# One transpose instead of two for the score maxima of a batch, and two VectorE additions in place of one

## The reference, cut to what matters

```python
v = (ctx @ Wv + bv); k = (ctx @ Wk + bk); q = (layernorm(x) @ Wq + bq)   # each cut into 16 heads of 16
energy = einsum('nqhd,nkhd->nhqk', q, k)
energy = where(mask == 0, neg, energy)
attn = softmax(energy / sqrt(16), axis=-1)
out = einsum('nhqk,nkhd->nqhd', attn, v).reshape(N, 128, 256) @ Wo + bo
x = x + tanh(g_xattn) * out
x = x + tanh(g_ffn) * tanh(layernorm(x) @ weight @ aux1 @ aux2 + bias)
```

## Time and profile before

| | |
|---|---|
| time, median of 3 runs | 1120.8 us (1119.55 to 1123.22) |
| span of the profiled execution, first to last instruction | 1118.3 us |
| TensorE busy | 1073.6 us, 96% of the span, 18979 products and transposes |
| VectorE busy | 966.1 us, 86% |
| ScalarE busy | 826.3 us, 74% |
| GpSimd busy | 774.2 us, 69% |
| granted TensorE clock, mean over the span | 0.988 of full speed |

### The profile page before, as it was taken

How to read it: one execution, slowest core, us unless ns; L and a number is a source line. 1 busy time by engine, 2 the same in 40 slices (tenths; PEclk the granted TensorE clock), 3 DMA queues, 4 the chain that set the end, 5 groups by cost and what they waited for, 6 DMA issues and landing times.

```text
span 1118.3 us, 45477 instructions
## 1 busy us (share of the span) xinstructions
PE 1073.6 (96%) x18979; PEld 941.8 (84%) x18979; DVE 966.1 (86%) x1272; ACT 826.3 (74%) x1275; POOL 774.2 (69%) x1185
## 2 busy tenths in 40 slices
PE   5989999999999999999999999999999999999975
PEld 4777888888888888888888888888888888888865
DVE  4788888988988988898888898898889889889876
ACT  4465877877887787787777787778778778777842
POOL 5245677777777776776777777777777777777653
PEclk9899999999999999999999999999999999999997
DMA  6134344334434433433433443443443344343232
GB/s 167 30 89 117 77 120 136 102 106 134 110 114 119 128 107 107 135 108 98 136 103 104 136 108 112 123 124 106 112 135 106 102 135 108 113 121 108 71 116 77
DMA packets 160189, 124.78 MB, mean 112 GB/s; under 512 B 91889, under 2 KB 126962, under 8 KB 159986
## 3 DMA queue, kind: packets, MB, share of 16 engines
q1 hardware_dynamic: 159842, 121.61, 38.8%
q10 hardware_dynamic: 144, 0.26, 0.1%
HBM read 69.41 MB, written 51.38 MB: 108 GB/s over the span
## 4 chain that ended last, share of the span: by engine, by line
PE 89%; DVE 5%; issue 2%; SPq 2%; DMA 1%; ACT 0%; DVEq 0%
PE ps_m L455 17%; PE ps_m L448 16%; PE ps_s L573 13%; PE ps_s L546 12%; PE ps_x L585 11%; PE ps_m L510 8%; PE ps_m L442 5%; PE ps_s L552 4%; PE ps_x L563 2%; DVE neg_max L938 2%; DVE probs L949 2%; DMA a_rows<-scratch_a 0%; DMA den<-a_den 0%; SPq L200 0%; PE ps_m L598 0%
## 5 line engine op out<-in xcount | busy, mean ns | idle before, releaser
L949 DVE TENSOR_TENSOR probs<-ps_s,far_T 128x2048 f32<-128x2048 f32 x128 | 293.3, 2292 | 36.8 <-PE ps_s L573 36.6
L938 DVE TENSOR_REDUCE neg_max<-ps_s 128x16 f32<-128x2048 f32 x128 | 291.3, 2276 | 6.4 <-PE ps_s L552 6.3
L748 ACT ACTIVATE probs<-probs 128x2048 f32<-128x2048 f32 x128 | 244.5, 1910 | 7.9 <-DVE probs L949 7.7
L723 ACT ACTIVATE q_aug<-ps_m,q_bias,q_scale 128x256 f32<-128x256 f32 x256 | 123.7, 564 | 161.9 <-PE ps_m L448 152.4
L573 PE MATMUL ps_s<-q_aug,k_aug 32*128 32x128 f32 x4096 | 152.8, 284 | 7.4 <-DVE neg_max L938 3.3
L546 PE MATMUL ps_s<-k_aug,q_aug 32*128 32x128 f32 x4096 | 151.1, 284 | 6.4 <-DVE probs L949 6.1
L573 PEld LDWEIGHTS ps_s<-q_aug,k_aug 32*128 32x128 f32 x4096 | 129.9, 187 | 27.2 <-issue 17.4
L944 DVE TENSOR_TENSOR q_aug<-q_aug,ps_x 128x512 f32<-128x512 f32 x128 | 88.0, 687 | 74.0 <-PE ps_x L563 74.0
L546 PEld LDWEIGHTS ps_s<-k_aug,q_aug 32*128 32x128 f32 x4096 | 126.9, 187 | 28.3 <-issue 28.3
L585 PE MATMUL ps_x<-probs,v_ones 128*32 128x128 f32 x4096 | 139.2, 277 | 3.9 <-issue 2.3
L388 POOL TENSOR_TENSOR y<-y,th 128x512 f32<-128x512 f32 x58 | 74.1, 1278 | 88.7 <-ACT th L769 88.7
(11 more groups left out here) (122 smaller groups left out, 1958.2 us busy)
## 6 DMA issues: line engine op xcount, KB each, us to landing
scratch_a<-a_den SPq DMA_DIRECT2D x64, 512.0 KB, 3.1
x_in<-in_x SPq DMA_DIRECT2D x64, 256.0 KB, 3.7
a_rows<-scratch_a SPq DMA_DIRECT2D x64, 256.0 KB
den_wide<-scratch_r SPq DMA_DIRECT2D x64, 256.0 KB
out<-y SPq DMA_DIRECT2D x64, 256.0 KB, 5.3
ctx_in<-in_ctx SPq DMA_DIRECT2D x252, 64.0 KB, 3.8
den<-a_den SPq DMA_DIRECT2D x128, 8.0 KB
scratch_r<-den_r SPq DMA_DIRECT2D x64, 16.0 KB, 1.4
```

The lines of the kernel that those rows point to most:

```text
L723: last = nc.scalar.activation(dst[:, :, 2 * m + a, :], src[:, m * TOK:(m + 1) * TOK].rearrange("p (n q) -> p n q", q=P), ACT.Identity, bia ...
L748: nc.scalar.activation(tile, tile, ACT.Exp).then_inc(probs_ready, 1)
L938: nc.vector.tensor_reduce(out_v, ps_s[:], AX.X, ALU.max, negate=True).then_inc(max_ready, 1)
L949: nc.vector.tensor_tensor(probs[i % 2][:].rearrange("p j s q -> p (j s) q"), ps_s[:].rearrange("p j s q -> p (j s) q"), far_T[:].unsqueeze ...
```

## The change

What it does: `maxima` writes each maximum twice, once for each parity, at the two places of `neg_max` where one transpose brings it to the spare rows of both; its input is viewed as (j, m, a, k) and its output as (j, m, a) with strides 32, 1 and 16. `turn_max` is one transpose into `ps_x[:, 0]`. A row of it holds data for the slots of one parity only, so that `append_max` becomes two VectorE instructions of 128x256, one for each parity: the turned rows times a column of zeros and ones (`parity`, one value per partition), plus the query slots of this parity. Each of the two raises `q_ready2`, and the two waits on it count double. For the rows to meet, the heads of a row group change slots: parity a now has slot 2m + 1 - a in `spread`, in `heads_of` and in the order in which `weigh_values` writes `ps_x`. Beyond the transposes taken away and the additions split, the order on the engines stays as it was, and SP's list is the same.

```diff
-        neg_max = [sb(f"neg_max{i}", [P, D + P]) for i in range(2)]
+        neg_max = [sb(f"neg_max{i}", [P, P]) for i in range(2)]
...
-            return [(j, (slot // 2) * 2 * G + 2 * j + slot % 2) for j in range(G)]
+            return [(j, (slot // 2) * 2 * G + 2 * j + 1 - slot % 2) for j in range(G)]
...
-                for a in range(2):
-                    last = nc.tensor.transpose(ps_x[:, a, :], neg_max[i % 2][:, a * D:a * D + P], ident[:])
-                last.then_inc(max_turned, 1)
+                nc.tensor.transpose(ps_x[:, 0, :], neg_max[i % 2][:], ident[:]).then_inc(max_turned, 1)
...
             def scores_T(i):
-                pe.wait_ge(q_ready2, i + 1)
+                pe.wait_ge(q_ready2, 2 * (i + 1))
...
             def weigh_values(i):
-                pe.wait_ge(q_ready2, i + 3 if i < NB - 3 else min(i + 2, NB))
+                pe.wait_ge(q_ready2, 2 * (i + 3 if i < NB - 3 else min(i + 2, NB)))
...
-                        last = nc.tensor.matmul(ps_x[j * ROWS:(j + 1) * ROWS, s, :], v_ones[p % V_RING][:, n, h, :],
+                        last = nc.tensor.matmul(ps_x[j * ROWS:(j + 1) * ROWS, s + 1 - 2 * (s % 2), :], v_ones[p % V_RING][:, n, h, :],
...
             def spread(dst, src, scale, bias, ready):
-                        last = nc.scalar.activation(dst[:, :, 2 * m + a, :], src[:, m * TOK:(m + 1) * TOK].rearrange("p (n q) -> p n q", q=P),
+                        last = nc.scalar.activation(dst[:, :, 2 * m + 1 - a, :], src[:, m * TOK:(m + 1) * TOK].rearrange("p (n q) -> p n q", q=P),
...
             def maxima(i):
-                out_v = neg_max[i % 2][:, D:].rearrange("p (j c) -> p j c", j=G)[:, :, 0:SLOTS]
-                nc.vector.tensor_reduce(out_v, ps_s[:], AX.X, ALU.max, negate=True).then_inc(max_ready, 1)
+                out_v = neg_max[i % 2][:].rearrange("p (j a c) -> p j c a", j=G, a=2)[:, :, 0:KT, :]
+                nc.vector.tensor_reduce(out_v, ps_s[:].rearrange("p j (m a) k -> p j m a k", a=2), AX.X, ALU.max,
+                                        negate=True).then_inc(max_ready, 1)
...
             def append_max(i):
                 dve.wait_ge(max_turned, i + 1)
-                q = q_aug[i // 2 % 2][:, i % 2].rearrange("p (m a) q -> p m (a q)", a=2)
-                rows = ps_x[:, 0:2, :].rearrange("p a q -> p (a q)").unsqueeze(1).to_broadcast([P, KT, 2 * P])
-                nc.vector.tensor_tensor(q, q, rows, ALU.add).then_inc(q_ready2, 1)
+                slots = q_aug[i // 2 % 2][:, i % 2].rearrange("p (m a) q -> p a m q", a=2)
+                rows = ps_x[:, 0:1, :].to_broadcast([P, KT, P])
+                for a in range(2):
+                    nc.vector.scalar_tensor_tensor(slots[:, a], rows, parity[:, a:a + 1], slots[:, a], ALU.mult,
+                                                   ALU.add).then_inc(q_ready2, 1)
```

More of the change, by code:

```diff
@@ L857, in setup_spreads @@
                     for a in range(2):
-                        last = nc.vector.tensor_reduce(one_row[:, m, a:a + 1], columns[:, 2 * m + a + D * (1 - a), :], AX.X, ALU.add)
+                        last = nc.vector.tensor_reduce(one_row[:, m, a:a + 1], columns[:, m + D * (1 - a), :], AX.X, ALU.add)
                 last.then_inc(spreads_ready, 1)
```

## The result

The change makes the kernel a little slower: 1126.1 us (median of 8 runs, 1122.0 to 1131.3) against 1121.1 us (8 runs, 1119.6 to 1123.2), a ratio of 1.0046 with a 95% interval of 1.0025 to 1.0068. The forecast was 1128.8 us with a range of 1122.5 to 1138. Measured again later, the same kernel took 1130.2 us against 1121.9 us, a ratio of 1.0062 (1.0041 to 1.0083).

The account below looks back on a forecast made before the run. VectorE's chain from `append_max` to `maxima` was taken to bound 115 halves: +9.2 us, less 1.3 for 12 halves bound by the scores, plus 0.1 for the last batch, +8.0 together, giving 1128.8 us, range 1122.5 to 1138.

Parts of the forecast that it names:

- What bounds it: Before the change, VectorE's chain from `append_max` to `maxima` bounds 115 halves, the scores 12; 0.15 us handover to `scores_T`.
- half B: Second half of a two-batch pair, from one turning of the maxima to the next; 7.93 us before the change.
- half A: First half of a two-batch pair, turning to turning, its `append_max` followed by `low_of_x`; 8.47 us before the change.
- One transpose fewer: In `turn_x` on TensorE: `append_max` may start 0.30 instead of 0.41 us after the turning, -0.11 us per half.
- Two additions: On VectorE, two of 256 at 0.40 us each replace one of 512 at 0.61: 0.80 us, +0.19 per half.
- `maxima` at nothing: VectorE's reduction, same 2048 elements read, 16 results spaced otherwise: no cost, 0.03 us either way, 3.5 us for the range.
- The sum: Whole kernel: +0.08 us for 115 VectorE-bound halves, -0.11 for 12 score-bound, last batch +0.1; together +8.0 us, 1128.8 us.
- What is late next: After the change VectorE bounds by more; scores behind the mask addition slip 0.04 us, inside the available room.
- TensorE is the bound: Rival for the whole kernel: the saved transpose counts fully, 0.11 us x 127 = 14 us saved, 1106.8 us; chance 0.05.
- The column is read for free: Rival on VectorE's split addition: two cost 0.68 us, -0.04 per VectorE-bound half, 1114.9 us, faster; chance 0.10.
- Each instruction pays its whole fixed part: Rival on VectorE's split addition: 0.16 us fixed part, column nothing, +0.05 per VectorE-bound half, 1125.3 us; chance 0.10.
- The second addition does not overlap: Rival on VectorE: the second addition starts only after the first ends, +0.16 us per half, 1138 us; chance 0.07.

Follow-up runs that it names:

- the reordered change: The change with statistics of x moved behind add_residual and moments of y in front of the additions on VectorE, against the change: 1105.0 us, again 1106.0 us.
- the two additions alone: The kernel before, both transposes kept, its one addition split into two of 128x256 times a 0/1 column: 1140.0 us, ratio 1.0159 to the kernel before.

## Why the prediction was right

*What bounds it.* Right for the changed kernel: VectorE's list from the additions to the maxima sets both halves, and taking other pieces off it gains 0.35 us a pair. For the kernel before it is right in half B alone, where 0.06 us could be gained on VectorE. In half A taking 0.33 us off the list gained nothing. There `maxima` started as soon as the scores were through and `scores_T` when TensorE came to it, while VectorE's own list would have let it start only some 0.03 us earlier. The count of 115 halves bound by VectorE took the gap of 0.15 us as proof, and in half A that gap stands there by luck.

*One transpose fewer, -0.11 us a half.* Right: the additions start 0.31 us after the turning, forecast 0.30.

*Two additions, +0.19 us, 0.80 in all.* Right: 0.79 against 0.605 us, +0.19. The row with the same width, source and kind of operand gave the value, where a price by element count alone (0.68) would have given the wrong sign; the run without the column shows that sign.

*`maxima` at nothing, 0.03 us either way.* The output pattern costs nothing. In all traces the reduction lasts 2.29 us where it starts as soon as the scores are through, and where it starts later 2.27 to 2.28 us in half A and 2.26 in half B. So the reduction of half A got 0.02 us shorter. That the longer ones count some waiting as work is an argument, not shown.

*The sum.* A pair 16.52 us instead of the 16.56 forecast; with 0.12 for 0.16 us a pair the regular part is 57 x 0.12 - 1.3 = +5.5 us instead of +8.0. The measured medians lie at +5.0 and, the second time, at +8.3. The term that was too large is the net of a half, +0.08: it is 0.08 in half B and 0.05 in half A. VectorE's list grew by 0.08 in both, but in half A it had been 0.03 us ahead of TensorE: 0.42 + 1.54 + 2.27 + 0.15 = 4.38 us, an estimate from the medians, against the 4.41 at which `scores_T` started. The sum came out near because the three paths of half A were so close, not because VectorE's was the last. The profiled execution came to +7.8 us of span only because its irregular gaps are 2.6 us longer in sum; that it meets the forecast of +8.0 is chance.

*What is late next.* Right for the scores behind the mask addition: they start 0.25 us after the turning (533.47), forecast 0.24, inside the room. Wrong for TensorE: there were not about 0.10 us of hidden waiting per half but none in half A and 0.06 in half B. The step that failed is "The last of twelve starts 11 x 0.119 = 1.31 us after the first". It starts 1.41 us after the first, since the first step alone takes 0.22, and from there `scores_T` comes 0.21 us later, as the scores do behind a transpose (0.20). The difference between `make_f` (1.43 us) and `make_o` (1.61) is these two longer steps and no wait. The sum did not use this number, since both sides of it became earlier by the same transpose. The expectation of the reordered change missed by 0.25 us a pair for other reasons: `maxima` starts 1.90 and 1.85 us after the turning and not 1.80, since the scores need 1.65 us where I had taken 1.55; the reduction lasts 2.29 us; and in half B TensorE arrives last.

*The rivals.* "TensorE is the bound" falls for half B and for the changed kernel, by the two additions alone; in half A of the kernel before TensorE did arrive last, with VectorE 0.03 us ahead of it. "The column is read for free" falls by the run without it, 0.67 against 0.79 us, as long as the price is the column's. "Each instruction pays its whole fixed part" falls by the same run, where the split costs 0.06 us, not 0.16; that it lands near the measured time of the change is two errors that cancel, the split too dear and the column free. "The second addition does not overlap" falls by 0.79 us for the two.

## What to carry to other kernels

Where two engines take turns on one buffer, a short wait hides in the tail of the instruction in front: an engine that is 96% busy may still start each piece the moment another lets it. The gap from the releaser's end to the waiter's start, compared with a place where the wait is plain, is a first test, but it cannot tell a wait from two paths of the same length: here it was 0.15 us in half A, where nothing waited, and in half B, where something did. The start of the waiter's last instruction in front is the better reading, and a piece taken off the releaser's list decides it. If the releaser is the path or close to it, a cheaper instruction on the busy engine pays only as long as the releaser does not get longer for it. Before trading work between engines, look at what stands on the releaser's list between its input and the awaited result, and move out what nobody needs there: here that was worth 24 us in the changed kernel (20 of them in the regular pairs), and it turned the change's loss of 8 us into a gain of 7.

## What the runs showed that I had not expected

Multiplying by a per-partition column and adding costs VectorE 0.06 us more than a plain addition or maximum, at both widths seen (0.67 against 0.61 at 512 elements, twice 0.40 against twice 0.34 at 256), also when the same small tile was read by the instruction in front.

On TensorE the change between kinds of products costs time on both sides. From the last full-size product of 256 columns to the first of 32 rows it takes 0.21 us, from a transpose of 128 to it 0.20, against 0.12 and 0.11 within their groups; and the first full-size product behind products of 32 rows stands 0.22 us ahead of the second. Even steps over a whole group give a wait that is not there.

In every execution single pairs are longer, by up to 3.2 us, beside gaps of 0.3 to 1.6 us on TensorE with no releaser in the profile, 2 to 8 us in sum. They stand at the same pairs in kernels whose lists are alike: three of the five longest are the same in the two executions of the change, and all five longest of the first are among the six longest of the reordered change. The transfers of the instruction queue in front of them are told above. What they come from was not tried; they are as large as the effect studied here, which is why the regular pair is the better measure.
